# Conditioned mixture kernel: id-free loads first, lora factors over 64 rows, language merges in one block, last round's outputs wait for VectorE

## What is computed

```python
# 1. conditioning: for each sequence b, weights wi, wo plus common and chosen low-rank parts
h   = relu(x @ wi.T + 2*(x@ca_i.T)@cb_i.T + 2*(x@A_i[id[b]].T)@B_i[id[b]].T)      # 128 -> 512
c   = h @ wo.T + 2*(h@ca_o.T)@cb_o.T + 2*(h@A_o[id[b]].T)@B_o[id[b]].T            # 512 -> 128
# 2. mixture: 4 rounds over 4 experts
cur = c
for r in range(4):
    logits = cur @ Wg[r] + bg[r]
    cw = softmax over the top 2 of 4, else 0
    cur = cur + sum_e cw[e] * (gelu(cur @ W1[e] + b1[e]) @ W2[e] + b2[e])
x = x + cur
# 3. language: z = (x @ A_l[lang[b]].T) @ B_l[lang[b]].T + emb[lang[b]], rank 16
# 4. feed forward of z: silu gate, two hidden layers 512x512, back to 128; added to x
```

## Time and profile before

| | us |
|---|---|
| median of 3 runs | 491.57 |
| lowest, highest | 490.34, 491.91 |
| the profiled execution | 491.71 |
| its span in the trace | 489.7 |
| PE busy in the span | 481.3 (98%) |
| DVE, ACT busy | 401.5, 391.8 |
| POOL busy | 121.0 |

### The profile page before, as it was taken

One profiled execution on the slowest core, in us unless ns is written; L12 is line 12 of the kernel. 1 busy time (PEld: TensorE's weight loads), 2 busy tenths in 40 slices (PEclk: granted clock), 3 DMA queues, 4 the chain that ended last, 5 costly groups with the idle time before them and its releaser, 6 DMA issues.

```text
span 489.7 us, 7440 instructions
## 1 busy us (share of the span) xinstructions
PE 481.3 (98%) x2262; PEld 396.2 (81%) x2262; DVE 401.5 (82%) x638; ACT 391.8 (80%) x542; POOL 121.0 (25%) x105
## 2 busy tenths in 40 slices
PE   7999999999999999999999999999999999999996
PEld 6799788888888888888888888888887887788885
DVE  2798899999999999999899999989997658644343
ACT  2878989798898788888888878888887888597653
POOL 4997122121222122121212121231313144400000
PEclk9999999999999999999999999999999999999999
DMA  7701612020202012020202021220202000000001
GB/s 176 245 4 64 255 48 88 2 88 0 88 1 86 20 66 86 1 86 0 86 0 86 1 86 60 70 88 0 86 2 86 1 1 0 1 0 1 0 21 68
DMA packets 6698, 26.30 MB, mean 54 GB/s; under 512 B 2194, under 2 KB 2578, under 8 KB 4498
## 3 DMA queue, kind: packets, MB, share of 16 engines
q1 hardware_dynamic: 5618, 21.20, 12.0%
q0 software_dynamic: 528, 3.67, 2.2%
q10 hardware_dynamic: 528, 1.11, 0.9%
HBM read 24.81 MB, written 1.18 MB: 53 GB/s over the span
## 4 chain that ended last, share of the span: by engine, by line
PE 84%; DVE 6%; issue 3%; ACT 2%; POOL 2%; DMA 1%; ACTq 1%; DVEq 0%
PE bank L479 30%; PE bank L480 30%; PE bank L483 22%; DVE hid_lo L1070 1%; POOL ffn_lo L390 1%; DMA cur<-cond_base 1%; PE bank L565 1%; PE bank L564 1%; DVE prod L1081 1%; ACT act_out L776 1%; PE bank L497 0%; ACT moe_hi L927 0%; DVE bank L1012 0%; DVE wins L1008 0%; POOL cur L442 0%
## 5 line engine op out<-in xcount | busy, mean ns | idle before, releaser
L776 ACT ACTIVATE act_out<-bank,vec 128x512 f32<-128x512 f32 x256 | 163.2, 681 | 45.9 <-PE bank L483 24.6
L1070 DVE TENSOR_TENSOR hid_lo<-act_out,hid_hi 128x1024 fp32r<-128x1024 f32 x128 | 160.9, 1278 | 23.2 <-ACT hid_hi L781 23.1
L781 ACT ACTIVATE hid_hi<-act_out 128x1024 fp32r<-128x1024 f32 x128 | 135.9, 1062 | 8.1 <-ACT act_out L776 0.4
L444 POOL TENSOR_TENSOR cur<-cur,prod 128x512 f32<-128x512 f32 x48 | 65.5, 1365 | 239.6 <-DVE prod L1081 239.1
L479 PE MATMUL bank<-hid_hi,moe_hi 128*128 128x512 f32 x256 | 100.1, 391 | 0.9 <-POOL cur L444 0.9
L479 PE MATMUL bank<-xhi,moe_hi 128*128 128x512 f32 x256 | 99.7, 390 | 0.0
L483 PE MATMUL bank<-hid_hi,moe_lo 128*128 128x512 f32 x256 | 99.7, 390 | 0.0
L480 PE MATMUL bank<-hid_lo,moe_hi 128*128 128x512 f32 x256 | 99.7, 389 | 0.0
L480 PE MATMUL bank<-xlo,moe_hi 128*128 128x512 f32 x256 | 99.6, 389 | 0.0
L483 PE MATMUL bank<-xhi,moe_lo 128*128 128x512 f32 x256 | 99.6, 389 | 0.0
L479 PEld LDWEIGHTS bank<-hid_hi,moe_hi 128*128 128x128 f32 x256 | 48.1, 188 | 12.9 <-POOL cur L444 1.3
(11 more groups left out here) (119 smaller groups left out, 576.8 us busy)
## 6 DMA issues: line engine op xcount, KB each, us to landing
cw_all<-cw_dram SPq DMA_DIRECT2D x16, 1024.0 KB, 4.6
stage<-ffn_w POOLq DMA_DIRECT2D x1, 2304.0 KB, 9.5
cw_all<-moe_w SPq DMA_DIRECT2D x4, 512.0 KB, 9.1
stage<-lora_all SPq DMA_DIRECT2D x6, 160.0 KB, 5.3
x<-x_t POOLq DMA_DIRECT2D x3, 256.0 KB, 6.9
out_t<-x SPq DMA_DIRECT2D x3, 256.0 KB, 2.5
cur<-cond_base ACTq DMA_DIRECT2D x2, 256.0 KB, 5.3
stage<-ffn_w POOLq DMA_DIRECT2D x1, 512.0 KB, 4.0
```

The lines of the kernel that those rows point to most:

```text
L444: pool.tensor_tensor(cur[:, c, :], cur[:, c, :], prod[:, s % 2, :], ALU.add).then_inc(add_done, 1)
L776: act.activation(act_out[:, f // 2, f % 2, :], bank[:, f, :], ACT.Gelu_apprx_tanh, bias=vec[:, V_B1 + e * FC + f:V_B1 + e * FC + f + 1]).t ...
L781: act.activation(hid_hi[:, s % 2, 2 * pr:2 * pr + 2, :], act_out[:, pr, :, :], ACT.Copy)\
L1070: dve.tensor_tensor(hid_lo[:, s % 2, 2 * pr:2 * pr + 2, :], act_out[:, pr, :, :], hid_hi[:, s % 2, 2 * pr:2 * pr + 2, :].bitcast(F32), ALU ...
```

## The change

Five things:

1. ACT's queue issues `cond_base` kind 0, x of chunk 0 and `cond_base` kind 1 before anything that needs the ids. POOL's three loads of x wait for the factors of batch 3 instead of batch 1.
2. A batch's factors are laid out as 64 rows of 640 numbers, kind 0 in the first 32 rows and kind 1 in the next, instead of 32 rows of 1280. The bytes are the same.
3. The two language halves lie in rows 0 to 15 and 32 to 47, and one `merge_lang` behind the last piece of `expert_in` multiplies both, half by half in turn. There is none in the middle of the prologue.
4. The prologue's order is rewritten on PE, ACT, DVE and POOL; PE takes the merges of batches 4 and 5 earlier, kind 0 before `cond_hidden(1)` and kind 1 before `cond_out(0)`. Every operation but the language blocks is there as often as before. `WARM` is 12 instead of 15.
5. In the last round (where n is a plain number) `expert_out` waits on `prod_done`, DVE's count, instead of `add_done`.

```diff
-LORA_W = D + F + F + D
-FIRST_BANKS = (6, 7, 4, 5, 2, 3)
-LATER_BANKS = (6, 7, 5)
+LORA_W = D + F
...
+MERGE_GROUPS = (((0, 0), (1, 0)),
+                ((0, 1), (1, 1)),
+                ((2, 0), (3, 0)),
+                ((2, 1), (3, 1)),
+                ((4, 0), (5, 0)),
+                ((4, 1), (5, 1)),
+                ((6, 0), (7, 0)),
+                ((6, 1), (7, 1)))
+MERGED = tuple(m for group in MERGE_GROUPS for m in group)
+MERGE_BANKS = (6, 7, 4, 5, 2, 3, 6, 7, 5, 6, 7, 5, 6, 7, 5, 6)
+SUMS = ((0, 0), (1, 0), (0, 1), (2, 0), (1, 1), (2, 1), (3, 0), (3, 1), (4, 0), (5, 0), (4, 1), (5, 1), (6,
...
-WARM = 15
+WARM = 12
...
-        lang_f = [stage[:, 2 * LORA_W + i * 8 * D:2 * LORA_W + (i + 1) * 8 * D].rearrange("p (b n) -> p b n", n=2 * D)
-                  for i in range(2)]
+        lora = stage[:, 0:4 * LORA_W].rearrange("p (h n) -> p h n", h=4)
+
+        lang_raw = stage[:, 4 * LORA_W:4 * LORA_W + 8 * D].rearrange("p (b n) -> p b n", n=2 * D)
+        lang_f = [lang_raw[2 * RANK * i:2 * RANK * i + RANK, :, :] for i in range(2)]
         mer_hi = ffn_hi[:, 0:2 * AHEAD, :].rearrange("p (b m) f -> p b m f", m=2)
         mer_lo = ffn_lo[:, 0:2 * AHEAD, :].rearrange("p (b m) f -> p b m f", m=2)
         moe_raw = cw_all[:].rearrange("p s e t -> p s (e t)")
...
-        def lora_rows(b):
-            return slice(32 * (b % 4), 32 * (b % 4) + 2 * RANK)
+        def lora_rows(b, kind):
+            first = 2 * RANK * (2 * (b % 2) + kind)
+            return slice(first, first + 2 * RANK)
 
         def merged(b, kind):
...
-            queue.dma_start(lora[lora_rows(b), b // 4, :],
+            queue.dma_start(lora[4 * RANK * (b % 2):4 * RANK * (b % 2 + 1), b // 2, :],
                             lora_all[bass.ds(e, 1), :, :].rearrange("e r n -> (e r) n")).then_inc(lora_in[b], 16)
 
...
-                sp.dma_start(lang_f[b // 4][0:RANK, b % 4, :],
+                sp.dma_start(lang_f[b // 4][:, b % 4, :],
                              lang_lora[bass.ds(e, 1), :, :].rearrange("e r n -> (e r) n")).then_inc(lang_in, 16)
                 sp.dma_start(emb[:, b:b + 1],
...
-            pool.wait_ge(lora_in[1], 16)
+            pool.wait_ge(lora_in[3], 16)
             for c in range(1, CHUNKS):
...
-            def merge_pair(j):
-
-                p, kind = MERGE_PAIRS[j]
-                free = max(summed_in(merge_bank(2 * j + i), 2 * j) for i in range(2))
+            def merge_group(j):
+
+                group = MERGE_GROUPS[j]
+                first = sum(len(g) for g in MERGE_GROUPS[:j])
+                free = max(summed_in(merge_bank(first + i), first) for i in range(len(group)))
                 if free:
                     pe.wait_ge(merge_free, free)
-                pe.wait_ge(lora_in[2 * p], 16)
-                pe.wait_ge(lora_in[2 * p + 1], 16)
-                for fc in range(FC if kind else 1):
-                    for i in range(2):
-                        rows, half, at = lora_rows(2 * p + i), p // 2, merge_bank(2 * j + i)
-                        if kind == 0:
-                            mm = pe.matmul(bank[:, at, :], lora[rows, half, 0:D], lora[rows, half, D:D + F],
-                                           start=True, stop=True)
-                        else:
-                            a = D + F + fc * P
-                            mm = pe.matmul(bank[:, at, fc * D:(fc + 1) * D], lora[rows, half, a:a + P],
-                                           lora[rows, half, D + 2 * F:LORA_W], start=True, stop=True)
-                        if fc == (FC - 1 if kind else 0):
-                            mm.then_inc(merge_done, 1)
-
-            def merge_lang(half):
-                if half == 0:
-                    pe.wait_ge(merge_free, summed_in(lang_bank(0), len(MERGED)))
-                else:
-                    pe.wait_ge(cw_done, 1)
+                for b in sorted({b for b, kind in group}):
+                    pe.wait_ge(lora_in[b], 16)
+                for fc in range(FC):
+                    for i, (b, kind) in enumerate(group):
+                        factors, at = lora[lora_rows(b, kind), b // 2, :], merge_bank(first + i)
+                        if kind == 0 and fc == 0:
+                            pe.matmul(bank[:, at, :], factors[:, 0:D], factors[:, D:D + F],
+                                      start=True, stop=True).then_inc(merge_done, 1)
+                        elif kind == 1:
+                            mm = pe.matmul(bank[:, at, fc * D:(fc + 1) * D], factors[:, fc * P:(fc + 1) * P],
+                                           factors[:, F:F + D], start=True, stop=True)
+                            if fc == FC - 1:
+                                mm.then_inc(merge_done, 1)
+
+            def merge_lang():
+
+                pe.wait_ge(merge_free, summed_in(lang_bank(0), len(MERGED)))
+                pe.wait_ge(cw_done, 1)
                 pe.wait_ge(lang_in, 32 * BATCHES)
                 for j in range(4):
-                    factors = lang_f[half][0:RANK, j, :]
-                    mm = pe.matmul(bank[:, lang_bank(half), j * D:(j + 1) * D], factors[:, 0:D], factors[:, D:2 * D],
-                                   start=True, stop=True)
-                mm.then_inc(merge_done, 1)
+                    for half in range(2):
+                        factors = lang_f[half][:, j, :]
+                        mm = pe.matmul(bank[:, lang_bank(half), j * D:(j + 1) * D], factors[:, 0:D], factors[:, D:2 * D],
+                                       start=True, stop=True)
+                        if j == 3:
+                            mm.then_inc(merge_done, 1)
 
             def first_logits(c):
                 if c == 0:
...
-                pe.wait_ge(add_done, n + 1)
+                if isinstance(n, int):
+                    pe.wait_ge(prod_done, n - 1)
+                else:
+                    pe.wait_ge(add_done, n + 1)
                 for fc in range(FC):
                     if fc % 2 == 0:
...
-            merge_pair(0)
-            merge_pair(1)
-            merge_pair(2)
-            merge_pair(3)
+            merge_group(0)
+            merge_group(1)
+            merge_group(2)
+            merge_group(3)
             cond_hidden(0)
+            merge_group(4)
             cond_hidden(1)
-            merge_pair(4)
+            merge_group(5)
             cond_out(0)
-            merge_pair(5)
+            cond_hidden(2)
             cond_out(1)
-            cond_hidden(2)
-            merge_pair(6)
+            merge_group(6)
             cond_hidden(3)
-            merge_pair(7)
+            merge_group(7)
+            cond_hidden(4)
+            first_logits(0)
             cond_out(2)
-            first_logits(0)
-            cond_hidden(4)
             cond_out(3)
             cond_hidden(5)
-            merge_lang(0)
             cond_hidden(6)
             cond_out(4)
             cond_out(5)
             cond_hidden(7)
             first_logits(1)
             expert_in(0, 0, 0, (0,))
+            cond_out(6)
             expert_in(0, 0, 0, (1,))
-            cond_out(6)
+            cond_out(7)
             expert_in(0, 0, 0, (2,))
-            cond_out(7)
-            merge_lang(1)
             expert_in(0, 0, 0, (3,))
+            merge_lang()
             pe.wait_ge(moe_lo_done, MOE_PIECES)
             with pe.Fori(0, ROUNDS - 1) as rnd:
                 round_steps(rnd, False)
...
 
+            base_load(act, 0)
             x_load(act, 0)
+            base_load(act, 1)
             act.wait_ge(const_done, 1)
             act.activation(low_any[0:1, :], blank[0:1, 0:1], ACT.Gelu_apprx_tanh)
             act.wait_ge(ids_in, 16)
             lora_load(act, 1)
-            base_load(act, 0)
             lora_load(act, 3)
-            base_load(act, 1)
             x0_high(0)
             merged_high(0, 0)
             merged_high(1, 0)
             merged_high(0, 1)
```

112 lines of the change are left out of this document (55 added, 57 removed).

## The result

The changed kernel takes **492.7 us** (median of 22 executions, 489.54 to 494.9) against 490.33 of the kernel before on the same chip (22, 489.42 to 493.82): a ratio of 1.0037, 95% interval 1.0023 to 1.0051. It is slower, by 2.4 us between the medians and 1.8 us by the ratio, and outside the forecast range of 487.2 to 490.2. The profiled execution is one of 493.04 us; its span is 491.0 against 489.7. The 491.57 from which the forecast started was the median of three executions, 1.2 above this one of 22.

A forecast was written before the change was run, and what follows sets the result against it. PE was taken to bound the kernel, POOL and DVE close behind in the prologue. Gains of 2.3 us there and 1.1 in the last round, off the profiled 491.71, gave 488.3, forecast as 488.2 us, range 487.2 to 490.2.

The forecast's parts named there:

- the last round: Last round's output product: waiting on DVE's read instead of POOL's addition removes PE's 1.04 us stall, gaining 1.1 us.
- 2.3 was taken: Prologue gain of 2.3 us, range 0.9 to 3.0, with DVE deciding; PE alone would be 2.8 us earlier.
- The first merge: Prologue, PE's first merge on batch 1's factors: 0.1 us later, range 0.6 earlier to 1.3 later.
- the sum 768/180 = 4.3 us: Prologue DMA: ACT's three early loads, 768 KB at 180 GB/s, take 4.3 us from 1.8 on, to 6.1.
- The first rival: Moderately late front queue: batch 1's factors about 1.0 us later, at 8.3, shifting the prologue; 489.2 us, chance 0.15.
- The point at which the text called itself wrong: Prologue sign in the trace after: the forecast is wrong if the first merge is past 8.5.
- the third rival: The clock falls in PE's 1.7 us rest before its first merge: 1.8 us lost, 490.0 us, chance 0.03.
- The other ends: Prologue ends besides PE's: POOL not before 44.0, 2.1 us earlier; DVE's second `hidden_low` at 49.2, 2.4 us earlier.
- the fourth rival: ACT's new order makes POOL or DVE wait; only about 0.8 us of prologue gain arrives; 490.1 us, chance 0.13.
- nothing is charged: POOL's prologue chain: may idle 0.6 us before it costs anything; charge zero, 0 to 0.8 for the range.
- The two earlier gaps: Prologue: PE's waits of 0.45 us before the third merge and 0.63 before `cond_hidden(1)` go, 1.1 us in sum.
- 1.5 was summed for them: Prologue on PE: reordered merges gain 0.4 us, and joining the language merges removes one block, 1.1 us.

The follow-up runs named there:

- the second (8.15): The changed kernel repeated word for word on another chip, against the kernel before: 493.1 us, ratio 1.0039.

## Why the prediction was wrong

The forecast was 488.2, the time is 492.7. Against the kernel before on the same chip it was 3.4 us less, and is by the ratio 1.8 more: 5.2 us are missing. By the runs they fall into four parts: 2.4 for the clock (ratio 1.0037 to 0.9988 with 24 warming matmuls), 0.7 to 0.9 for POOL's moved wait (to 0.9973), 0.3 for the rest of the loads with the longer warming (1.5 below the kernel before becomes 1.8, both at 0.999 or 1.000), and 1.6 that even then, with the loads of before and the clock up, is not there. Of these 1.8 the last round has 1.1, so the prologue has 0.7 where 2.3 was taken. The steps compare kernels on different chips, each with the kernel before beside it, so none is better than a few tenths.

**The first merge** was forecast for 7.4, in a range up to 8.7, and came at 8.56. In the other profiled runs with these loads and a warming that had ended it came at 8.15 to 9.24, in those with the loads of before at 6.61 to 7.32: they do not overlap, and the loads cost it 1 to 2 us. The step that failed is the sum 768/180 = 4.3 us: it gave the three loads the whole DMA until 6.1. The DMA was faster than that, 249 GB/s where 180 was taken. What was left out is the share that SP's factors take of it, and so the third load was in at 7.5 and batch 1's factors at 8.4. The first rival had the size (8.3), at 0.15, but by a slow pace, 150 GB/s, which the trace does not show; it priced it at 1.0 us. The point at which the text called itself wrong, 8.5, was met by the first profile and not by the second (8.15), which lost as much. The prediction named from the Trainium skill (DMA: Bandwidth & Descriptors, Queues, rings and completion order) that the descriptors of one queue are taken in ring order and that queues take turns. The trace agrees with both: ACT's four loads landed in their order of issue, and SP's went on beside them.

**The clock** was the third rival, with 0.03 and 490.0. This is the step that decided. Its argument, that the trace of before has no fall after 0.95 us, was a single execution at a single length. The rest grew to 2.88, not to the 1.7 it took; the 1.7 has the shorter warming in it but not the late factors, and the two were never added. (Its own sum is off too: six records at 12 per microsecond are 0.5 us, which ends the warming at 5.87 and not at 5.7. It ended at 5.68.) And the loss was sized by the 3.6 us of the first warming; the clock stayed at half for 10.2 us, from 8.04 to 18.27. And `WARM` 12 was costed at nothing "so long as the clock stays up", which was the question. The trace after, where the clock went to 0.50 after 2.4 us of rest, agrees with the Trainium skill's sentence (TensorE: Matmul & The Clock Gate, Part 1) that idleness throttles the engine again.

**POOL** was taken to start at 9.97 "as before". Here the working missed an instruction of the diff: the wait on `lora_in[3]` stands ahead of POOL's three x issues of 1.95 us together, and behind those stand its 27 low parts, which have almost no slack. Batch 3's factors land later than batch 1's, so the issues moved from 7.49 to 9.87 and the chain with them. (In the changed kernel ACT's high part came last, 0.33 us behind the issues; with `WARM` 24 it was the issues.) It was neither costed nor bounded.

**The other ends.** DVE was forecast to decide the prologue. It was POOL, in every run with the new order, with 0.82 to 0.88 us of waiting in the profiled executions at the loop's entry: the fourth rival's mechanism. By the trace this is the larger part of the 1.6 us, as PE entered the loop at 46.19 in the run with the loads of before, 1.2 earlier than before and not 2.3. The step that failed is "nothing is charged" for POOL's end: it was allowed 0.6 us of idling before it costs anything, and idled 1.9 in that run, so that it ended at 45.94 and not by 44.6. A later wait, of 0.28 to 0.34 us, is in all these runs as well and stood in no sum: the first output product's wait for POOL's memset behind DVE. No run made POOL's end earlier, so what stands behind it is not known. The two earlier gaps behaved as forecast, the third merge and `cond_hidden(1)` no longer wait; but at a low clock that is no gain, and with the clock up (`WARM` 24) PE waits 0.44 and 0.74 us nearby instead.

**Right, with their sizes:** the last round (1.1 forecast, 1.1 measured); the language block's own duration (1.1 forecast, 1.16); 64 rows (zero, 0.3 either way; the interval goes from -1.2 to 0.0 us, so it does not tell zero from a gain of 1). The order and the language block together are worth some 0.4 us at a full clock (489.28 with 64 rows and `prod_done` at 0.999 or more, 488.91 with the order too), where 1.5 was summed for them; some 0.2 of the 0.4 are the language block.

## What to carry to other kernels

When an edit lets TensorE rest longer before its first real work, add up every edit that lengthens that rest, and give the clock a chance that a single undisturbed trace can't take away; look at the granted clock of all executions, not of the one profiled. When a wait is moved on an engine's queue, list what stands behind it, the issues and then the chain that has no slack, before anything else is costed. Loads that can start early are not free: they take the DMA from the one load that everybody waits for. To say when a load lands, count the bytes of all queues that are moved until then, not only those ahead of it in its own.
